# Folding the attention scale and the sign of the maxima into other instructions, in a transformer layer on eight cores

## The reference

```python
# x: (16, 2048, 1024), H = 16 heads of Dh = 64
def _L0_attn_ref(x, w_qkv, b_qkv, w_out, b_out):
    qkv = x @ w_qkv.T + b_qkv
    q, k, v = jnp.split(qkv, 3, axis=-1)      # each to (b, H, t, Dh)
    ...
    q, k = _rope(q, k)                        # rotates pairs by position
    scores = jnp.einsum('bhtd,bhsd->bhts', q, k) / jnp.sqrt(jnp.float32(Dh))
    scores = jnp.where(causal, scores, -jnp.inf)
    probs = jax.nn.softmax(scores, axis=-1)
    out = jnp.einsum('bhts,bhsd->bhtd', probs, v)
    ...
    return out @ w_out.T + b_out

x = x + _L0_attn_ref(_layernorm(x), ...)
x = x + _L0_ffn_ref(_layernorm(x), ...)       # two 512x512 matrices, real and imaginary
```

## Time and profile before

| What | Value |
|---|---|
| Median of 3 runs (lowest, highest) | 4630.61 us (4625.35, 4640.43) |
| The profiled execution's own time | 4625.56 us |
| Its span on the slowest core, core 5 | 4624.0 us |
| Spans of the 8 cores | 4607.9 to 4624.0 us |
| Mean granted clock of PE | 0.622 to 0.625 of full speed |
| Busy share: PE, DVE, ACT, POOL | 64%, 62%, 41%, 3% |

### The profile page before, as it was taken

How to read it: one execution, slowest core, us unless ns; L and a number is a source line. 1 busy time by engine, 2 the same in 40 slices (tenths; PEclk the granted TensorE clock), 3 DMA queues, 4 the chain that set the end, 5 groups by cost and what they waited for, 6 DMA issues and landing times.

```text
span 4624.0 us, 70849 instructions; the slowest of 8 cores (4607.9 to 4624.0 us)
## 1 busy us (share of the span) xinstructions
PE 2943.7 (64%) x15058; PEld 1506.0 (33%) x15058; DVE 2871.2 (62%) x10818; ACT 1890.6 (41%) x5448; POOL 149.6 (3%) x292
## 2 busy tenths in 40 slices
PE   3235543566778888885642555345677888888665
PEld 1012231233344455542211224113334445544222
DVE  4346546777777778772224563677777777777322
ACT  0120003455566667771113000344556666777211
POOL 0000000000000000000000000000000000000000
PEclk9997765555555555567775777555555555556777
DMA  0221110000000000001122112000000000000111
GB/s 3 64 69 32 37 55 3 3 3 3 3 3 3 3 3 2 3 2 60 55 78 78 37 33 64 3 3 3 3 3 3 3 3 3 2 3 3 46 56 46
DMA packets 76974, 101.30 MB, mean 22 GB/s; under 512 B 7780, under 2 KB 61172, under 8 KB 75543
## 3 DMA queue, kind: packets, MB, share of 16 engines
q1 hardware_dynamic: 63768, 75.78, 5.4%
q0 software_dynamic: 12800, 20.99, 1.3%
HBM read 75.77 MB, written 16.78 MB: 20 GB/s over the span
## 4 chain that ended last, share of the span: by engine, by line
DVE 44%; PE 19%; ACT 16%; issue 14%; DMA 4%; DVEq 2%; ACTq 0%; SPq 0%; POOL 0%; POOLq 0%
DVE mxl L664 11%; DVE pt L811 6%; ACT pt L742 4%; PE pb L1061 4%; ACT pt L754 4%; PE pb L555 3%; ACT mxl L765 3%; PE pb L967 3%; ACT pt L726 3%; DVEq L115 2%; DVE mxl L794 2%; DMA wbf<-wqkvT 2%; PE pb L496 2%; PE pb L637 2%; DVE scd L678 2%
## 5 line engine op out<-in xcount | busy, mean ns | idle before, releaser
L840 PE MATMUL pb<-identS,pt 128*128 128x128 bf16 x4352 | 591.3, 300 | 494.8 <-ACT ptT L852 271.5
L726 ACT ACTIVATE pt<-pb,mxl 128x512 bf16<-128x512 f32 x768 | 527.6, 687 | 720.4 <-DVE mxl L671 674.5
L874 PE MATMUL pb<-ptT,V 128*64 128x128 bf16 x4352 | 553.9, 308 | 329.9 <-ACT ptT L852 329.8
L637 PE MATMUL pb<-KO,QO 32*128 32x512 bf16 (+3 forms) x1280 | 695.5, 551 | 0.0
L637 PE MATMUL pb<-KE,QE 32*128 32x512 bf16 (+3 forms) x1280 | 691.0, 540 | 0.1
L852 ACT ACTIVATE ptT<-pb 128x512 bf16<-128x512 bf16 (+3 forms) x1280 | 614.9, 520 | 69.4 <-PE pb L840 61.2
L874 PEld LDWEIGHTS pb<-ptT,V 128*64 128x64 bf16 x4352 | 440.6, 165 | 598.7 <-issue 598.5
L840 PEld LDWEIGHTS pb<-identS,pt 128*128 128x128 bf16 x4352 | 389.9, 130 | 672.4 <-issue 652.3
L754 ACT ACTIVATE pt<-scd,mxl 128x128 bf16<-128x128 f32 x512 | 203.9, 398 | 824.7 <-DVE mxl L700 806.6
L664 DVE TENSOR_REDUCE mxl<-pb 128x1 f32<-128x512 f32 x768 | 529.4, 689 | 11.0 <-PE pb L637 4.3
L811 DVE TENSOR_SCALAR pt<-pt,mxl 128x512 bf16<-128x512 bf16 (+3 forms) x1664 | 408.3, 304 | 58.5 <-DVE mxl L794 4.2
(11 more groups left out here) (94 smaller groups left out, 3400.6 us busy)
## 6 DMA issues: line engine op xcount, KB each, us to landing
xtinS<-x SPq DMA_DIRECT2D x64, 512.0 KB, 3.5
wbf<-wqkvT SPq DMA_DIRECT2D x48, 512.0 KB, 4.0
y<-x3b POOLq DMA_DIRECT2D x32, 512.0 KB, 2.9
woF<-woutT SPq DMA_DIRECT2D x8, 1024.0 KB, 4.9
On<-ost POOLq DMA_DIRECT2D x256, 16.0 KB, 1.7
t_th_sin_hi<-th_sin_hi SPq DMA_DIRECT2D x2, 1024.0 KB, 6.8
t_th_sin_lo<-th_sin_lo SPq DMA_DIRECT2D x2, 1024.0 KB, 10.1
t_th_cos_hi<-th_cos_hi SPq DMA_DIRECT2D x2, 1024.0 KB, 13.2
```

The source lines that it names most:

```text
L637: tt=tt, Qb=Qb, Kb=Kb, eo=eo: e.matmul(pb[bk][0:128, 0:w_], Qb.ap()[32 * hm:32 * hm + 32, T * jb + 128 * tt: T * jb + 128 * tt + 128], Kb. ...
L726: par=par, mi=mi: e.activation(out=ptil[par].ap()[:, SPW * s_: SPW * s_ + w_], in_=pb[bk][0:128, 0:w_], func=AF.Exp, scale=0.125, bias=ml. ...
L840: e.transpose(bank[0:128, 128 * j:128 * j + 128], ptil[par].ap()[:, SPW * s_ + 128 * j: SPW * s_ + 128 * j + 128], ident.ap()),
L874: e.matmul(pb[pvb][0:64, 0:128], Vsb.ap()[:, 1024 * c + 64 * hh: 1024 * c + 64 * hh + 64], ptT[par].ap()[:, 128 * c:128 * c + 128], start= ...
```

## The change

Three things are moved. The factor 0.125 leaves the exponentials and goes into the weights and bias of q: for chunks 0 to 3 the cast (L471) becomes a multiplication by 0.125 with the same input and output. The partial maxima are reduced with a sign turned (`negate=True`), so that a maximum serves as the bias of its exponential as it is, and the instructions L671, L690 and L700 go away. Behind the last partial maximum one new instruction turns all of them back, for the total maximum and the factors. The exponentials read their bias in columns 0 to 5 and now wait for the reduce itself.

```diff
+        bcq = S.add("vector",
+                    lambda e: e.tensor_scalar(bcols.ap()[:, 0:8],
+                                              bcols.ap()[:, 0:8], 0.125,
+                                              None, ALU.mult),
+                    wait=[("s_ld", nld)], inc="s_cst")
...
+                    if wch < 4:
+                        S.add("vector",
+                              lambda e, wpar=wpar, wh=wh: e.tensor_scalar(
+                                  bass.AP(wbuf_b[wpar], 128 * wh,
+                                          [[2048, 128], [256, 8], [1, 128]]),
+                                  wbuf_f.ap(), 0.125, None, ALU.mult),
+                              wait=[("s_wld", S.now("s_wld"))] + gate,
+                              inc="s_wcast")
+                    else:
...
                           lambda e, ml=ml, mi=mi, bk=(b0 + s_) % 4,
                           w_=widths[s_]: e.reduce_max(
                               ml.ap()[:, mi:mi + 1], pb[bk][0:128, 0:w_],
-                              AX.X),
-                          wait=wg + [("s_sc", sc0 + s_ + 1)] if (wg or True)
-                          else (), inc="s_chv")
+                              AX.X, negate=True),
+                          wait=wg + [("s_sc", sc0 + s_ + 1)], inc="s_mx")
                     wg = []
-                    S.add("vector",
-                          lambda e, ml=ml, mi=mi: e.tensor_scalar(
-                              ml.ap()[:, 6 + mi:7 + mi], ml.ap()[:, mi:mi + 1],
-                              -0.125, None, ALU.mult),
-                          wait=[("s_chv", S.now("s_chv"))], inc="s_mx")
...
                 S.add("vector",
                       lambda e, ml=ml, mi=mi, sc_=sc_: e.reduce_max(
-                          ml.ap()[:, mi:mi + 1], sc_.ap(), AX.X),
-                      wait=[("s_chv", cpc)], inc="s_chv")
-                S.add("vector",
-                      lambda e, ml=ml, mi=mi: e.tensor_scalar(
-                          ml.ap()[:, 6 + mi:7 + mi], ml.ap()[:, mi:mi + 1],
-                          -0.125, None, ALU.mult),
-                      wait=[("s_chv", S.now("s_chv"))], inc="s_mx")
+                          ml.ap()[:, mi:mi + 1], sc_.ap(), AX.X, negate=True),
+                      wait=[("s_chv", cpc)], inc="s_mx")
                 mi += 1
                 nmx = mi
                 r["nmx"] = nmx
                 S.add("vector",
+                      lambda e, ml=ml, nmx=nmx: e.tensor_scalar(
+                          ml.ap()[:, 6:6 + nmx], ml.ap()[:, 0:nmx], -1.0,
+                          None, ALU.mult),
+                      wait=[("s_mx", mx0 + nmx)], inc="s_chv")
+                S.add("vector",
                       lambda e, ml=ml, nmx=nmx: e.reduce_max(
-                          ml.ap()[:, 24:25], ml.ap()[:, 0:nmx], AX.X),
+                          ml.ap()[:, 24:25], ml.ap()[:, 6:6 + nmx], AX.X),
                       wait=[("s_chv", S.now("s_chv"))], inc="s_chv")
                 S.add("vector",
                       lambda e, ml=ml: e.tensor_scalar(
-                          ml.ap()[:, 25:26], ml.ap()[:, 24:25], -0.125,
+                          ml.ap()[:, 25:26], ml.ap()[:, 24:25], -1.0,
                           None, ALU.mult),
                       wait=[("s_chv", S.now("s_chv"))], inc="s_mx")
...
                                     in_=pb[bk][0:128, 0:w_], func=AF.Exp,
-                                    scale=0.125,
-                                    bias=ml.ap()[:, 6 + mi:7 + mi],
+                                    bias=ml.ap()[:, mi:mi + 1],
...
-                          out=ml.ap()[:, 18:18 + nmx], in_=ml.ap()[:, 0:nmx],
-                          func=AF.Exp, scale=0.125, bias=ml.ap()[:, 25:26]),
+                          out=ml.ap()[:, 18:18 + nmx],
+                          in_=ml.ap()[:, 6:6 + nmx],
+                          func=AF.Exp, bias=ml.ap()[:, 25:26]),
```

More of the change, by code:

```diff
@@ L469, in emit_batch @@
                                 ("s_vmm", S.now("s_vmm"))]
-                    S.add("vector",
[L471 to L476, removed]
+                    if wch < 4:
[8 more added lines that the diff above has]
+                        S.add("vector",
+                              lambda e, wpar=wpar, wh=wh: e.tensor_copy(
+                                  bass.AP(wbuf_b[wpar], 128 * wh,
+                                          [[2048, 128], [256, 8], [1, 128]]),
+                                  wbuf_f.ap()),
+                              wait=[("s_wld", S.now("s_wld"))] + gate,
+                              inc="s_wcast")
                 ncast = S.now("s_wcast")
@@ L516, in emit_batch @@
                             wr.append(("s_ld", nld))
+                            wr.append(("s_cst", bcq))
                         pE = pb[2 * ppar][0:128, 0:SPW]
@@ L686, in stage_a @@
                           e.reduce_max(ml.ap()[:, mi:mi + 1],
-                                       pb[lb][0:128, 0:doff], AX.X),
-                          inc="s_chv")
-                    S.add("vector",
-                          lambda e, ml=ml, mi=mi: e.tensor_scalar(
-                              ml.ap()[:, 6 + mi:7 + mi], ml.ap()[:, mi:mi + 1],
-                              -0.125, None, ALU.mult),
-                          wait=[("s_chv", S.now("s_chv"))], inc="s_mx")
+                                       pb[lb][0:128, 0:doff], AX.X,
+                                       negate=True),
+                          inc="s_mx")
                     mi += 1
@@ L756, in stage_a @@
                                              dbase + doff + 128],
-                          in_=sc_.ap(), func=AF.Exp, scale=0.125,
-                          bias=ml.ap()[:, 6 + mi:7 + mi],
+                          in_=sc_.ap(), func=AF.Exp,
+                          bias=ml.ap()[:, mi:mi + 1],
                           accum_out=ml.ap()[:, 12 + mi:13 + mi]),
```

## The result

The changed kernel takes 4443.4 us in the median of 8 runs (4441.3 to 4463.8), the kernel before 4628.8 in 8 runs beside it: a ratio of 0.9604, 95% interval 0.959 to 0.9619. The forecast was 4440, with a range of 4380 to 4510. The profiled execution of the changed kernel had its longest span, 4455.5 us, on core 7; the other seven lie between 4427.9 and 4439.7. I therefore read core 5, the core of the trace before: 4439.7 us against 4624.0, 184 us less.

The account below looks back on a forecast made before the run. The prediction took a loop between DVE and ACT, repeated in each unit, as the bound: 4625.6 - 180 (shorter units) - 10 (clock) = 4436, put at 4440 us because the median lies 5 us above the profiled execution; range 4380 to 4510.

Parts of the forecast that it names:

- DVE and ACT bound each unit by one loop: Tile 13 unit, kernel before: 4.44 us from first reduce to L765 plus 2.84 unchanged make the whole 7.28 us period.
- Two reduces 0.61 apart: Full spans on DVE: without negations, reduces overlap by 0.08 us and start 0.61 apart instead of 0.90, 0.29 less.
- Rival 1: DVE's partial maxima: reduces don't overlap and stand 0.69 apart, -129 us and some clock, about 4500 us; chance 0.16.
- rival 3: DVE's partial maxima: each reduce holds the next like a dependent step, 0.79 apart, -55 us, 4571 us; chance 0.03.
- rival 4: DVE's reduces: the negation inside runs as a second, dependent pass, so slower, +133 us, 4759 us; chance 0.05.
- The tail, +0.12 us: End of each unit: the added turn-back makes last partial maximum to factor exponential 1.16 us instead of 1.04.
- Scores late from tile 8 on: Row tiles 8 to 15: PE's scores come one span per 0.85 us, so 0.90 can shrink to 0.85 only.
- Rival 5: All row tiles: PE's wait takes the place of DVE's, tile 13's period stays near 7.28 us; chance 0.02.
- Rival 2: Most of tiles 8 to 15: PE gets full clock, scores stop being late, -257 us, about 4365 to 4370; chance 0.08.
- PE's scores start 1.70 us after L765, so they move with it: Tile 13 unit: PE's next scores follow the factor exponential by 1.70 us, so its period falls to 6.70 us.
- The clock, -10: PE from tile 13 or earlier: denser matmuls bring some full clock, -10 us, a small part of 77.
- Edits at nothing: Exponentials' scale and bias constants, and 16 weight casts turned multiplications: no change in time, taken as 0.

Follow-up runs that it names:

- e8: Kernel before, with the score matmuls of the even half of each head left out (work left out): 4606.1 us, ratio 0.9946.
- e4: Kernel before, with the total maximum and its scaling replaced by one minimum, one DVE instruction less per unit: 4626.2 us, ratio 0.9990.
- e3: Changed kernel without the turn-back and L717, the total being one minimum over the negated maxima: 4379.8 us, ratio 0.9457 to the kernel before.
- e2: Changed kernel with each partial maximum and the masked copy made to wait for the maximum before: 4618.6 us, ratio 0.9977 to the kernel before.
- e9: Changed kernel with additional waits at the partial maxima and masked copy, for a semaphore value reached before attention: 4476.9 us, ratio 0.9671 to the kernel before.
- e7: Changed kernel with the score matmuls of the even half of each head left out (work left out): 4339.4 us, ratio 0.9370 to the kernel before.
- e5: Changed kernel with PE's first two transposes put ahead of the previous unit's value matmuls: 4429.5 us, ratio 0.9571 to the kernel before.
- e1: Kernel before with only the factor 0.125 folded into q's weights and bias, each negation kept: 4632.5 us, ratio 1.0004.
- e6: Changed kernel with both the shorter DVE tail (one minimum) and the new PE order: 4347.6 us, ratio 0.9390 to the kernel before.

## Why the prediction was right, point by point

*DVE and ACT bound each unit by one loop.* Shown for the kernel before, where e8 leaves some 23 us for PE's scores. e4 takes an instruction from DVE that is not on that loop: nothing. e3 takes two from the changed kernel that are: 64 us. e2 keeps DVE's work as short as the change made it and puts the dependence back: all but 10 us of the gain is gone.

*Two reduces 0.61 apart.* Right: 0.60 to 0.61 at an unchanged 688 ns. Rival 1 (0.69) and rival 3 (0.79) fall by this row, rival 4 by the unchanged durations. The Trainium skill (VectorE: DVE Perf Modes, "The DRAIN you can't avoid") has the next instruction start only when the pipe is empty, but the same section adds that one which is not held starts earlier, and the prediction told only the first half. The trace agrees with the second: with nothing held between them, the next instruction started 0.08 before the first had ended. The remark in that section of the Trainium skill that nothing is won by leaving out semaphores doesn't hold here: leaving the dependence out was worth 142 us (e2 against e9).

*The tail, +0.12 us.* It measured 1.16 to 1.19 from L701 to L768 (medians of the row tiles; 1.28 in tile 14), forecast 1.16. Tile 0 got slower by 0.13.

*Scores late from tile 8 on.* Right: 0.85 between reduces in tile 13, and e7 and e8 price the lateness, with PE's own loop in tiles 13 to 15, at 104 us after the change and some 23 before. Rival 5 is out: PE's wait ate part of the gain from tile 8 on, and tile 13 still went from 7.28 to 7.02. Rival 2 is out as well: tile 13's clock came to 0.53, and its scores still set 0.85 between reduces.

*PE's scores start 1.70 us after L765, so they move with it.* This is the one step that failed. In tiles 8 to 12 it held (1.12 us in tile 8 against 1.10 before). In tiles 13 to 15 the scores come 0.29, 0.30 and 0.22 us later after L768 than before after L765 (medians on core 5), and in tile 13 nothing made up for it. There the forecast left PE out as a bound of its own. Its row of scores, value matmuls, transposes and the wait for ACT to empty one of two transpose banks takes 7.02 us, more than the 6.70 of the DVE and ACT loop, so that tile gained 0.40 instead of 0.58 on the mean. e5 confirms it by hiding the copy under the value matmuls (6.74).

*The clock, -10.* In direction right: some full clock, which before began in tile 14, came in tile 13 on nearly every core, and now and then in tiles 11 and 12. Its size was not measured alone. Tiles 14 and 15 gained 0.06 and 0.24 us more than the steps at the lower clock gave, 10 us over their 32 units each; that this is the clock's doing is inferred from the granted clock of these tiles, 0.62 and 0.63 to 0.70 on core 5. Tile 13's miss (0.18) and tile 10's (0.05) took 7 us away. The total is as close as it is because these two nearly cancel, and that is luck.

*Edits at nothing.* Right: the multiplying cast 690 ns, and e1.

## What to carry to other kernels

A tiny instruction between two large independent ones costs not its own 154 ns but the break in the overlap: 0.29 us here. It waits for the instruction before it, so the next large one starts at 0.79 + 0.11 = 0.90 us instead of 0.61, though that one waits for nothing. Before pricing a removal, find which engine's row starts the instruction that closes the loop; one instruction less in DVE's tail was worth nothing before the change, and two less were worth 64 us after it. And write down the row of each engine that "merely follows", because the next bound may lie within 5% of the present one.

## What the runs showed of the hardware that I had not expected

A wait is an entry in DVE's queue of about 0.07 us. It is hidden while an earlier instruction runs (the units of tile 6 take 4.60 us with and without such waits, e9), but behind a wait that really holds it comes on top (0.47 instead of 0.40 us in e2). Waits that were long met cost 33 us in all at three places (e9).

A new order on PE with the same matmuls changed the granted clock of a row tile: over all cores and both sequences tile 14 has 0.60 to 0.66 in the changed kernel and 0.53 to 0.58 in e5, and with the shorter tail as well tile 12 goes from 0.50 to 0.56 up to 0.59 to 0.64 (e6). The order gained 14 us where the rows at one clock gave 30; that the clock took part of the rest was not shown by a run of its own.
